# Flamingo cross-attention and experts: first memsets placed behind the weights' split, key-stack transfers shared with ScalarE until scores begin

## What is computed

```python
def reference(x, ctx_2048, g_xattn, g_ffn, ...):
    # x: 32 x 100 x 256, ctx_2048: 32 x 1444 x 256
    x = x + tanh(g_xattn) * xattn(layernorm(x), ctx_2048, Wq, bq, Wk, bk, Wv, bv, Wo, bo)
    x = x + tanh(g_ffn) * ffn(layernorm(x), Wr, br, w1, b1, w2, b2, Wp1, bp1, Wp2, bp2)
    return x
# xattn: Q, K, V projections; 16 heads of 16; softmax(Q K^T / 4) V; Wo
# ffn: router over 12 experts, top 3; every expert 256 -> 640 -> 256 on its tokens,
#      results weighted and added per token; a gate from the mean over tokens
```

## Time and profile before

| | us |
|---|---|
| median of 3 runs | 2262.12 (2259.59 to 2262.18) |
| the profiled execution, its own time | 2268.39 |
| span of its profile | 2266.4 |
| TensorE busy | 2145.9 (95% of the span) |
| VectorE, ScalarE, GpSimd busy | 1411.2, 1160.2, 805.1 |

### The profile page before, as it was taken

The page is one execution under the profiler, slowest core; times in us unless marked ns, Lnnn a source line. Parts: engine busy times, 40 slices in busy tenths (PEclk is TensorE's granted clock), DMA queues, the critical chain, the costliest instruction groups (busy, mean ns, idle before and its releaser), DMA issues. The chain is left out here.

```text
span 2266.4 us, 61917 instructions
## 1 busy us (share of the span) xinstructions
PE 2145.9 (95%) x23554; PEld 1870.7 (83%) x23554; DVE 1411.2 (62%) x3223; ACT 1160.2 (51%) x2765; POOL 805.1 (36%) x1199
## 2 busy tenths in 40 slices
PE   5899999999999999999999999999995789999995
PEld 4688888888888888888888888888874678888884
DVE  4777777777777777777777777777763111111113
ACT  1366666666666666666566656666653223333331
POOL 4323433343344334333433443343311233333331
PEclk9999999999999999999999999999996899999997
DMA  5555555555555555555555555555532786887775
GB/s 135 148 137 148 137 137 140 134 136 144 137 133 134 139 143 140 139 140 134 134 143 137 136 133 137 148 136 139 130 107 58 207 266 187 221 222 218 213 213 169
DMA packets 253828, 345.07 MB, mean 152 GB/s; under 512 B 90296, under 2 KB 170652, under 8 KB 253404
## 3 DMA queue, kind: packets, MB, share of 16 engines
q1 hardware_dynamic: 221228, 303.28, 50.0%
q0 software_dynamic: 20256, 23.21, 5.4%
q10 hardware_dynamic: 12048, 14.63, 2.1%
HBM read 155.83 MB, written 42.86 MB: 88 GB/s over the span
## 5 line engine op out<-in xcount | busy, mean ns | idle before, releaser
L637 DVE TENSOR_REDUCE max_part<-max_ps 100x1 f32<-100x512 f32 (+1 forms) x1536 | 993.9, 655 | 355.1 <-PE max_ps L925 326.8
L513 ACT ACTIVATE probs<-score_ps 128x400 f32<-128x400 f32 x1498 | 733.4, 503 | 411.6 <-PE score_ps L908 402.9
L925 PE MATMUL max_ps<-k_stack,q_stack 96*100 96x512 f32 (+1 forms) x1536 | 597.4, 389 | 15.4 <-DVE max_part L637 14.9
L908 PE MATMUL score_ps<-q_stack,k_stack 97*128 97x200 f32 (+1 forms) x2996 | 599.2, 282 | 0.9
L908 PEld LDWEIGHTS score_ps<-q_stack,k_stack 97*128 97x128 f32 (+1 forms) x2996 | 464.2, 184 | 66.1 <-issue 30.4
L442 POOL TENSOR_TENSOR ctx_hi<-ctx_raw,zero_col 128x256 fp32r<-128x256 f32 (+1 forms) x384 | 213.6, 589 | 467.1 <-PE v_ps L939 433.7
L976 PE MATMUL pv_ps<-probs,v_ones 128*17 128x100 f32 x12288 | 304.9, 251 | 5.5 <-ACT pv_out L521 2.8
L976 PEld LDWEIGHTS pv_ps<-probs,v_ones 128*17 128x17 f32 x12288 | 257.5, 98 | 51.8 <-issue 39.0
L925 PEld LDWEIGHTS max_ps<-k_stack,q_stack 96*100 96x100 f32 x1536 | 257.2, 167 | 28.2 <-DVE max_part L637 23.6
L1300 ACT ACTIVATE hid<-h_ps,b_c 128x256 f32<-128x256 f32 x245 | 116.2, 474 | 311.0 <-PE h_ps L1424 305.2
L1211 POOL DMA_INDIRECT results_by_token<-y_t,slot x98 | 152.6, 1557 | 317.5 <-DVE y_t L1374 183.3
(11 more groups left out here) (192 smaller groups left out, 2351.3 us busy)
## 6 DMA issues: line engine op xcount, KB each, us to landing
k_stack<-k_hl SPq DMA_DIRECT2D x512, 128.0 KB, 2.6
w_raw<-in_w SPq DMA_DIRECT2D x98, 640.0 KB, 6.0
ctx_raw<-in_ctxT SPq DMA_DIRECT2D x64, 512.0 KB, 4.5
k_stack<-k_hl SPq DMA_DIRECT2D x512, 64.0 KB, 2.2
k_stack<-k_hl SPq DMA_DIRECT2D x256, 105.0 KB, 2.4
ctx_raw<-in_ctxT SPq DMA_DIRECT2D x32, 420.0 KB, 4.8
k_stack<-k_hl SPq DMA_DIRECT2D x256, 52.5 KB, 2.0
x_t<-rows_by_expert SPq DMA_DIRECT2D x49, 269.0 KB
```

The source lines that it names most:

```text
L513: act.activation(probs[0:tw, n % PROBS, :], score_bank(n)[0:tw, 0:UH * SQ], ACT.Exp, scale=SCALE).then_inc(exp_done, 1)
L637: dve.tensor_reduce(max_part[b % 2][:, h, j:j + 1], max_ps[m % 2][0:SQ, 0:CW[j]], AX.X, ALU.max).then_inc(max_read, 1)
L908: ins = pe.matmul(score_bank(n)[0:TW[i], 2 * SQ * p:2 * SQ * (p + 1)], k_stack[b % 2][:, 2 * u + p, 128 * i:128 * i + TW[i]], q_stack[b % ...
L925: pe.matmul(max_ps[m % 2][0:SQ, 0:CW[j]], q_stack[b % 3][0:96, h // 2, SQ * (h % 2):SQ * (h % 2) + SQ], k_stack[b % 2][0:96, h // 2, k0[j] ...
```

## The change

It moves work of the prologue and adds no arithmetic. VectorE now begins with the weights' split. The setting of v_ones0 and q_stack0 goes to slot -4, the wide bias copies to slot 2, q_stack1 and v_ones1 to slot 5, q_stack2, pv_ps, x_row and small to slot 7. The one semaphore for all of them becomes separate ones (v_ones_set, stack_ready, pv_zero), which ScalarE, SP and TensorE wait on. The four DMAs of ones go from SP's slot -1 to ScalarE's start. In the slots before 20, groups q 0 and 1 of each K half are issued by SP and groups 2 and 3 by ScalarE, at the end of the slot; from slot 20 on SP issues all.

```diff
@@ -225,6 +225,8 @@
         bias_ready = sem("bias_ready")
         const_row_ready = sem("const_row_ready")
         stack_ready = sem("stack_ready")
+        v_ones_set = sem("v_ones_set")
+        pv_zero = sem("pv_zero")
         setup = sem("setup")
         pool_setup = sem("pool_setup")
         ones_rows = sem("ones_rows")
@@ -283,6 +285,13 @@
 
         k0 = [128 * TPC * j for j in range(NC)]
 
+        def stack_keys(eng, b, j, o, some):
+            for q in some:
+                dst = k_stack[b % 2][:, 4 * o + q, k0[j]:k0[j] + CW[j]].bitcast(F32)
+                src = k_hl[32 * q:32 * q + 32, o, :, 0:CW[j]].bitcast(F32)
+                eng.dma_start(dst[0:64, :], src).then_inc(k_stacked[j][o], 16)
+                eng.dma_start(dst[64:96, :], src[:, 1, :]).then_inc(k_stacked[j][o], 16)
+
         N_TAIL = 4
         results = ys[1:1 + SLOTS, :].rearrange("(p i) d -> p i d", p=128)
 
@@ -343,18 +352,7 @@
 
                         wait(sp, k_read, KD * (NC * b + j) + o + 1)
                         wait(sp, score_done, UH * (NT * (b - 2) + TPC * (j + 1)))
-                        for q in range(4):
-                            dst = k_stack[b % 2][:, 4 * o + q, k0[j]:k0[j] + CW[j]].bitcast(F32)
-                            src = k_hl[32 * q:32 * q + 32, o, :, 0:CW[j]].bitcast(F32)
-                            sp.dma_start(dst[0:64, :], src).then_inc(k_stacked[j][o], 16)
-                            sp.dma_start(dst[64:96, :], src[:, 1, :]).then_inc(k_stacked[j][o], 16)
-                if g == -1:
-                    sp.wait_ge(const_ready, N_CONST)
-                    for p in range(2):
-                        row = k_stack[p][96:97, :, :].rearrange("p j t -> p (j t)").bitcast(F32)
-                        for i in range(2):
-                            sp.dma_start(row[:, ROW * ROW * i:ROW * ROW * (i + 1)],
-                                         ones[0:ROW, 0:ROW]).then_inc(ones_rows, 16)
+                        stack_keys(sp, b, j, o, (0, 1) if g < AT_SCORE else (0, 1, 2, 3))
                 b = batch_at(g, AT_XQ + 3)
                 if b is not None:
 
@@ -368,8 +366,8 @@
 
                     wait(sp, q_written, 16 * 4 * (b + 1))
                     wait(sp, score_done, NT * UH * (b - 2))
-                    if b == 0:
-                        sp.wait_ge(stack_ready, 1)
+                    if b < 3:
+                        sp.wait_ge(stack_ready, b + 1)
                     for e in range(2):
                         rows, cols = slice(HD * e, HD * e + HD), slice(SQ * e, SQ * e + SQ)
                         sp.dma_start(q_stack[b % 3][2 * HD * e:2 * HD * e + 2 * HD, :, cols].bitcast(F32),
@@ -513,6 +511,13 @@
                 act.activation(probs[0:tw, n % PROBS, :], score_bank(n)[0:tw, 0:UH * SQ],
                                ACT.Exp, scale=SCALE).then_inc(exp_done, 1)
 
+            act.wait_ge(const_ready, N_CONST)
+            for p in range(2):
+                row = k_stack[p][96:97, :, :].rearrange("p j t -> p (j t)").bitcast(F32)
+                for i in range(2):
+                    act.dma_start(row[:, ROW * ROW * i:ROW * ROW * (i + 1)],
+                                  ones[0:ROW, 0:ROW]).then_inc(ones_rows, 16)
+
             for g in range(FIRST, LAST):
                 b = batch_at(g, AT_POST)
                 if b is not None:
@@ -566,14 +571,21 @@
                 if b is not None:
                     wait(act, v_done, NT * b + i + 1)
 
-                    if b == 0 and i == 0:
-                        act.wait_ge(split_w, 1)
+                    if b < 2 and i == 0:
+                        act.wait_ge(v_ones_set, b + 1)
                     if b >= 2:
                         act.wait_ge(pv_done, visit_of(NT * (b - 2) + i) + 1)
                     act.activation(v_ones[b % 2][0:TW[i], i, :, 0:HD],
                                    v_ps[0:TW[i], 0:D].rearrange("p (h d) -> p h d", h=NH),
                                    ACT.Copy).then_inc(v_read, 1)
                 exps(g, 3)
+                for j in range(NC):
+                    for o in range(KD):
+                        b = batch_at(g, 4 * j + 2 * o)
+                        if b is not None and g < AT_SCORE:
+
+                            act.wait_ge(k_read, KD * (NC * b + j) + o + 1)
+                            stack_keys(act, b, j, o, (2, 3))
                 b = batch_at(g, AT_POST + 6)
                 if b is not None:
 
@@ -604,27 +616,21 @@
                 dve.wait_ge(setup, own[0])
 
 
-            dve.memset(pv_ps[:], 0.0).then_inc(setup, 1)
-            for p in range(3):
-                dve.memset(q_stack[p][:].bitcast(F32), 0.0).then_inc(setup, 1)
-            dve.memset(x_row[:], 0.0).then_inc(setup, 1)
-            dve.memset(small[:], 0.0).then_inc(setup, 1)
-            own[0] += 6
-            dve.wait_ge(setup, own[0])
             dve.wait_ge(kv_in, 32)
             for i in (1, 0):
                 link(dve.tensor_copy(w_hi[:, i], w_kv[:, i]))
                 link(dve.tensor_tensor(w_lo[:, i], w_kv[:, i], w_hi[:, i].bitcast(F32), ALU.subtract))
-            for p in range(2):
+            dve.sem_inc(split_w, 1)
+
+            def set_stack(p):
+                dve.memset(q_stack[p][:].bitcast(F32), 0.0).then_inc(stack_ready, 1)
+
+            def set_ones(p):
                 link(dve.memset(v_ones[p][:, :, :, HD:VW], 1.0))
 
                 link(dve.memset(v_ones[p][:, NT - 1], 0.0))
                 link(dve.memset(v_ones[p][0:TW[NT - 1], NT - 1, :, HD:VW], 1.0))
-            dve.sem_inc(split_w, 1)
-            dve.sem_inc(stack_ready, 1)
-            dve.wait_ge(weights_in, 16 * N_WEIGHTS)
-            link(dve.tensor_copy(bv_wide[:, 0, :], bv_c[:, 0:1].broadcast_to([128, SQ])))
-            dve.tensor_copy(bv_wide[:, 1, :], bv_c[:, 1:2].broadcast_to([128, SQ])).then_inc(bias_ready, 1)
+                dve.sem_inc(v_ones_set, 1)
 
             n_chain = [0]
 
@@ -650,6 +656,21 @@
             p_self = pr[:].unsqueeze(2).broadcast_to([SQ, NE, NE])
 
             for g in range(FIRST, LAST):
+                if g == AT_XQ + 1:
+                    set_ones(0)
+                    set_stack(0)
+                if g == CONST_SLOT - 1:
+                    dve.wait_ge(weights_in, 16 * N_WEIGHTS)
+                    link(dve.tensor_copy(bv_wide[:, 0, :], bv_c[:, 0:1].broadcast_to([128, SQ])))
+                    dve.tensor_copy(bv_wide[:, 1, :], bv_c[:, 1:2].broadcast_to([128, SQ])).then_inc(bias_ready, 1)
+                if g == CONST_SLOT + 2:
+                    set_stack(1)
+                    set_ones(1)
+                if g == CONST_SLOT + 4:
+                    set_stack(2)
+                    dve.memset(pv_ps[:], 0.0).then_inc(pv_zero, 1)
+                    link(dve.memset(x_row[:], 0.0))
+                    link(dve.memset(small[:], 0.0))
                 maxes(g, 0)
                 b = batch_at(g, AT_POST + 1)
                 if b is not None:
@@ -968,6 +989,8 @@
                 if first == 0:
 
                     wait(pe, v_read, NT * (b + 1))
+                    if b == 0:
+                        pe.wait_ge(pv_zero, 1)
                     wait(pe, pv_read, b)
                 for i in range(first, last + 1):
                     for u in range(4):
```

## The result

| | before | with the change |
|---|---|---|
| median | 2262.12 us | 2251.58 us |
| lowest to highest | 2259.59 to 2265.62 (7 runs) | 2250.84 to 2256.29 (7 runs) |
| profiled execution: own time, span | 2268.39, 2266.4 | 2253.91, 2252.2 |
| first K product | 18.91 | 15.10 |
| ScalarE's copy of the second chunk | 34.77 | 28.30 |

The change is faster by less than half of a per cent: the ratio of the times is 0.9958, 95% interval 0.9947 to 0.997, and 10.5 us lie between the medians. The forecast was 2252.3, its range 2246.5 to 2258.5.

What follows compares the result with a forecast made beforehand. From 100 to 500 us TensorE alone was taken to set the pace, so only earlier idle or slow-clock stretches could shrink. The terms -7.3 + 3.3 - 5.8 gave -9.8 us, from 2262.12 to 2252.3; range 2246.5 to 2258.5.

Steps and rivals of the forecast that it cites:

- Start: Program start up to the first K product: it comes 3.3 us earlier, with xT_q behind the four issues of ones.
- First keys: First key transfers: ScalarE's copy of the second chunk starts at 28.1, not 34.77, 6.7 us earlier, including the start's 3.3.
- First maximum: Start of the maxima: 7.3 us earlier, from 6.7 at the key copy, 2.3 of clock gained, 1.7 of issues lost.
- Slots 6 to 14: Slots where VectorE is 88% busy: 3.3 us given back, 2.2 for slot 7's memsets and 1.1 for ScalarE's issues.
- 15 to 19: Slots with batch 1's keys: 5.8 us gained, the 3.52 gap and 3.4 of slow clock less 1.1 for issues.
- An issue on ScalarE's queue: Price of one key transfer's issue on ScalarE before slot 20: 0.64 us, taken from SP's same transfers.
- The price of 1.47: Higher price per ScalarE issue, 1.47 us, taken from DMAs where both queues write to DRAM; kept for range and a rival.
- Nothing changes from 100 us on: Stretch from 100 us on: TensorE alone sets the pace, so what reaches it earlier ends earlier.
- The DMA engines: Rival at key copies: engines, not issue, set the landing; 0.9 us longer in ten slots, half shown, 2256.8; chance 0.18.
- ScalarE's queue: Rival: four issues take 5.9 us, delaying copies 3.3 in each of ten slots; half shown, 2269; chance 0.04.
- Doesn't reach the end: Rival: context loads and splits refill the gaps, or slow clock elsewhere takes the gain; time stays 2262; chance 0.05.
- more than forecast: Rival: slot 7's memsets fall into VectorE's 12% idle time and ScalarE's issues into its own; 2247; chance 0.07.

Runs made afterwards that it cites:

- the repeat: Kernel before and changed kernel, both unchanged, measured and profiled once more on one chip: 2262.84 and 2257.57 us, ratios 1.0004 and 0.9973.

## Why the forecast held

The time and the sign held, 0.7 us off the median, and 10.5 us at the first score against a forecast of 9.8. The mechanism held too: the memsets' move and the split of keys each pay by themselves, and the landing waits that the forecast named shrank or went. That the size is met to 0.7 us is in part luck. In the repeat the first score moved by 8.1 us (91.50 to 83.41) and the ratio 0.9973 stands for 6.1 us; and in the steps below errors of both signs cancel. By its steps:

- **Start, -3.3.** It came to -3.8. The mechanism is the forecast's, xT_q behind the ones and TensorE behind xT_q. The weights landed at 9.7 and not at 10.3, which the forecast had taken from before, and the four issues took 3.21, not 2.7. Without the ones GpSimd's split would have let K go at 13.9, as the forecast said, so they cost 1.2 by the trace and 0.7 by the run that moved them, not 1.7.
- **First keys, -6.7.** Measured from 34.77 to 28.30, -6.5. The landing that ends this wait is SP's share, issued from 23.26, as forecast to 0.2 us.
- **First maximum, -7.3.** Measured from 41.48 to 33.80, -7.7. In the repeat it was from 40.69 to 34.28, -6.4. What follows the copy, -0.6 in the forecast from -2.3 of clock and +1.7 of issues, so came to -1.2 and then to +0.1. Its two terms can't be told apart. ScalarE's first hold showed 1.92 us at TensorE (1.15 in the repeat), more than the 0.85 charged, but it lies ahead of the landing that is waited for in any case, and so does the slow stretch at 24 to 28. On the clock itself the forecast was wrong: it had no slow window after 24 us, and a clock near 0.5 between 28 and 80 us among its signs of being wrong. The first profile has a slow stretch at 24 to 28, and the repeat has them at 36 to 40 and 42 to 48. The gain didn't hang on it.
- **Slots 6 to 14, +3.3, and 15 to 19, -5.8.** Together -2.5, and -2.9 measured between first maximum and first score (50.69 before, 47.84 now), -1.7 in the repeat (50.81 and 49.13). Slot 7's memsets were charged at 2.2 and stopped TensorE for 2.16; what they add to the wait there is 1.5, by the run without them. The gap before 77.84 and the slow stretch behind it are gone.
- **An issue on ScalarE's queue, 0.64.** Measured 0.62 in the median, 0.57 to 0.86 in the first 82 us, with SP issuing at the same time. The price of 1.47, which would have turned the sign, belongs to the transfers of rows 8.
- **Nothing changes from 100 us on.** TensorE is busy 395.72 of 400 us, 98.9%, below the 99% that the forecast named as a sign of being wrong; before had 398.41, and the repeats have 398.97 and 396.44. So the share did fall a little, for a reason that stays open, but no time was lost: from first to last score it takes 1629.8 and 1627.3 us before, 1624.3 and 1628.4 with the change. The medians differ by what the first score moved, 10.5, and the profiled executions by 14.5; the 4 us between are in single executions and no part of the gain.

The rivals. **The DMA engines** did in part what the rival says: 92% busy, transfers 0.8 us slower, the copy at 33.75 waiting for a landing 5.3 us after its last issue went out at 28.46. But TensorE then idled 0.69 us for them, once (1.18 in the repeat), not 0.45 in each of ten slots. The Trainium skill says in "DMA: Bandwidth & Descriptors", section "Issuing engines are not separate DMA queues", that DMAs started by different engines share the same 16 DMA engines, and that a second issuing engine saves only the time to initiate them, usually small beside the transfer. The rows agree with the sharing: 0.92 busy, and 3.4 us to landing where it was 2.6. They don't agree with "small": eight issues take 5.12 us, and saving half of them, the split alone, made the kernel 0.28% faster. **ScalarE's queue** was the right mechanism at the wrong size of hold: 2.6 us per hold is nearly covered before scores begin, 5.1 us costs 0.9% (1.0055 against some 0.9966, the mean of the change's two ratios), about 20 us, near the 16.5 that the rival had for a hold of 5.9. **Doesn't reach the end** fell with the medians, and **more than forecast** with the 2.16 us for which the memsets of slot 7 stopped TensorE.

## What to carry to other kernels

Where one queue issues without pause and its landing is waited for, another engine's queue is worth its share, so long as that engine holds it for less than the others' work covers: find that length in the profile, and don't read it off the engine's busy share. The same four issues per copy that gained some 6 us in all (0.28%) while ScalarE waited for others anyway cost 0.72 us each time once exponentials were due. And a memset moved out of the start should go where its engine waits for something, not into the first stage that it bounds: the same memsets four and six slots earlier took 1.5 us off TensorE's wait.

## What the hardware showed that I hadn't expected

- Small transfers among the loads were dear. With four of 76 rows of 304 bytes, onto one partition, issued at 3.4 us, the last weights landed at 13.4 and not at 9.7. It was seen in one profile; that the transfers themselves hold up the others is the likely reading.
- The clock's lower level appears at different places in executions of the same kernel: 24 to 28 us in the one profile of the changed kernel, 36 to 40 and 42 to 48 in the other. Between 1.5 and 6.4 us went that way in the prologues of nearly all the kernels here, and 12.65 in the one whose TensorE idled most. A difference of 2 us in one profile's first score can be the clock alone.
- Issuing on two queues at once made neither slower: a median of 0.60 on SP (0.59 before) and 0.62 on ScalarE, with a few of 0.82 to 1.00 on both.
